# A decoder layer's cross-attention softmax taken in two halves of the batch

## What is computed

```python
def proj(x, W, bias):
    y = x @ W.T + bias
    return y.reshape(b, s, head_num, hd).transpose(0, 2, 1, 3).reshape(b * head_num, s, hd)
Q = proj(q, Wq, bq)
K = proj(k, Wk, bk)
V = proj(v, Wv, bv)
scores = jnp.einsum('bqd,bkd->bqk', Q, K) / jnp.sqrt(jnp.asarray(hd, jnp.float32))
attn = jax.nn.softmax(scores, axis=0)
res = jnp.einsum('bqk,bkd->bqd', attn, V)
out = res.reshape(b, head_num, s, hd).transpose(0, 2, 3, 1).reshape(b, s, hd * head_num)
```

## Time and profile before

| | us |
|---|---|
| median of 3 runs | 711.3 (708.06 to 711.74) |
| profiled execution | 712.35 |
| its span, first to last instruction | 710.6 |
| busy: PE / DVE / ACT / POOL | 652.4 / 557.7 / 460.2 / 419.3 |

### The profile page before, as it was taken

One profiled execution on the slowest core, in us unless ns is written; L12 is line 12 of the kernel. 1 busy time (PEld: TensorE's weight loads), 2 busy tenths in 40 slices (PEclk: granted clock), 3 DMA queues, 4 the chain that ended last, 5 costly groups with the idle time before them and its releaser, 6 DMA issues. The chain is left out here.

```text
span 710.6 us, 10958 instructions
## 1 busy us (share of the span) xinstructions
PE 652.4 (92%) x3298; PEld 450.0 (63%) x3298; DVE 557.7 (78%) x866; ACT 460.2 (65%) x1260; POOL 419.3 (59%) x366
## 2 busy tenths in 40 slices
...
DMA packets 29469, 56.46 MB, mean 79 GB/s; under 512 B 4705, under 2 KB 4961, under 8 KB 28898
## 3 DMA queue, kind: packets, MB, share of 16 engines
...
...
## 5 line engine op out<-in xcount | busy, mean ns | idle before, releaser
L1034 DVE SCALAR_TENSOR_TENSOR arena<-ps,arena 128x512 f32<-128x512 f32 x288 | 212.9, 746 | 16.7 <-PE ps L1382 4.7
L1382 PE MATMUL ps<-x_hi,w_sb 128*128 128x512 f32 x384 | 174.9, 455 | 16.9 <-DVE arena L1034 8.2
L1062 DVE SCALAR_TENSOR_TENSOR y<-ps,arena,y 128x512 f32<-128x512 f32 x192 | 138.9, 745 | 23.6 <-PE ps L1441 19.4
L1382 PE MATMUL ps<-x_lo,w_sb 128*128 128x512 f32 x384 | 154.2, 401 | 0.0
L1441 PE MATMUL ps<-heads_hi,wo_sb 128*128 128x512 f32 x256 | 110.6, 432 | 3.8 <-DVE y L1062 2.4
L754 ACT ACTIVATE arena<-ps,small 128x128 f32<-128x128 f32 x256 | 90.6, 377 | 36.2 <-DVE small L1040 36.2
L587 POOL TENSOR_TENSOR arena<-arena,consts 128x512 f32<-128x512 f32 x75 | 96.7, 1289 | 22.6 <-DMA arena<-arena 21.2
L581 POOL TENSOR_TENSOR arena<-arena,consts 128x512 f32<-128x512 f32 x75 | 96.8, 1291 | 22.2 <-DVE arena L1034 22.1
L1382 PEld LDWEIGHTS ps<-x_hi,w_sb 128*128 128x128 f32 x384 | 74.1, 193 | 51.4 <-issue 11.4
L605 POOL TENSOR_TENSOR y<-arena,y 128x512 f32<-128x512 f32 x64 | 82.4, 1288 | 39.4 <-ACT arena L795 37.3
L708 POOL TENSOR_SCALAR var_eps<-mean_var 128x2 f32<-128x2 f32 (+1 forms) x10 | 6.5, 647 | 166.0 <-DVE mean_var L1181 166.0
...
## 6 DMA issues: line engine op xcount, KB each, us to landing
arena<-arena SPq DMA_DIRECT2D x160, 128.0 KB, 2.3
...
```

Of the source, the lines that this page charges most:

```text
L1034: nc.vector.scalar_tensor_tensor(acc, group_bank(p, KC * c + g), scale_of(p // 2, c, g), acc, ALU.mult, ALU.add).then_inc(dve_scaled, 1)
L1062: nc.vector.scalar_tensor_tensor(dst, by_tile(out_bank(p, u)), out_scale_of(p // 2, u), dst, ALU.mult, ALU.add).then_inc(out_added, 1)
L1382: mm = nc.tensor.matmul(group_bank(p, u), w_sb[:, c, g, :], part[:, g, half * HALF:(half + 1) * HALF], start=(k == 0), stop=(k == 1))
```

## The change

Softmax in two halves. `maximum2(h)`, `shift(h)`, `add_exps(h)` do four batches. The first half is shifted by its own maximum. The second half's maximum is joined with the first's (a running maximum), and ACT makes one 128x128 factor `x_c`, the exponential of the difference, with which the first half's sum and, at the end, its inverse are multiplied. The two `tensor_reduce` of 2048 become `fold`: four `tensor_tensor` of 1024, 512, 256 and 128. PE no longer sums exponentials.

```diff
+            maximum2(0)
+            shift(0)
+            add_exps(0)
+            maximum2(1)
+            step(nc.vector.tensor_tensor(x_m[1], x_m[1], x_m[0], ALU.max))
+            nc.vector.tensor_tensor(x_c, x_m[0], x_m[1], ALU.subtract).then_inc(apart2_ready, 1)
+            shift(1)
+            dve.wait_ge(factor2_ready, 1)
+            step(nc.vector.tensor_tensor(x_s[0], x_s[0], x_c, ALU.mult))
+            add_exps(1)
+            step(nc.vector.tensor_tensor(x_s[1], x_s[1], x_s[0], ALU.add))
+            step(nc.vector.reciprocal(x_r[1], x_s[1]))
+            step(nc.vector.tensor_tensor(x_r[0], x_r[1], x_c, ALU.mult))
...
+            def fold(v, op, dst):
+
+                for n in (1024, 512, 256):
+                    step(nc.vector.tensor_tensor(v[:, 0:n], v[:, 0:n], v[:, n:2 * n], op))
+                step(nc.vector.tensor_tensor(dst, v[:, 0:P], v[:, P:2 * P], op))
```

```diff
+                        elif g == 0 and c in K2_TILES:
+                            wait_product_bank(f, f"G{KC * c}")
+                            channels_by_token(K2_TILES.index(c), wk2, ctx_t)
...
+                    elif c in K2_TILES:
+                        copy_k2(K2_TILES.index(c))
```

```diff
+            pe.wait_ge(out_added, DVE_TILES * QPK * 2 * NKV)
+            pe.wait_ge(part_added, QPK * 2 * NKV)
+            for n in range(KC):
+                turn_y(BPH + n)
+                next_unit(KC + n, wq2, x2_t)
+            pe.wait_ge(proj2_copied, 2 * KC)
             for b in range(BPH):
                 scores2(b)
+                turn_x(0, BPH + b)
+                next_unit(2 * KC + b, wk2, ctx_t)
+            pe.wait_ge(x_t_ready, NB)
+            for n in range(KC):
+                next_unit(3 * KC + n, wq2, x2_t)
...
+            for b in range(BPH):
+                scores2(BPH + b)
                 values(b)
+            for b in range(BPH, NB):
+                values(b)
```

```diff
+            copy_q2(12)
             exps2(0)
+            copy_q2(13)
+            seed_bias(0)
             exps2(1)
             exps2(2)
+            copy_q2(14)
+            seed_bias(1)
             exps2(3)
+            copy_q2(15)
+            seed_bias(2)
+            for b in range(BPH):
+                copy_scores2(BPH + b)
+                copy_v2(b)
+                seed_bias(b + 3)
+            act.wait_ge(apart2_ready, 1)
+            nc.scalar.activation(x_c, x_c, ACT.Exp, scale=XSCALE).then_inc(factor2_ready, 1)
```

354 lines of the change are left out of this document (176 added, 178 removed).

## The result

Of 20 runs of each kernel the median is 707.75 us (705.29 to 711.97) with the change and 710.83 us (706.88 to 714.39) before it. The ratio is 0.9962, 95% interval 0.9944 to 0.9981: a gain of 3.1 us, real but within the 0.5% that was called no change. The forecast was 702.2 us, so about 9 us of gain; a third of it came.

A forecast was written before the change was run, and what follows sets the result against it. Bound: PE's key and query units, then DVE's softmax, in a row, with DVE idle in the first. Span 710.6 - 10.1 + 1.0 = 701.5, plus 1.75 gives 703.25, less 1.05 gives 702.2 us; range 696.5 to 709.0.

The forecast's parts named there:

- Part 1: Last self-attention phase: four key units, 13.7 us of PE work, partly fill 3.5 us of gaps; phase ends 10.5 us later.
- Part 2: Last output products and first layer norm, `turn_y(0)` to `turn_y(4)`: 17.0 us, with DVE the slower engine at 14.3 us.
- Part 3: First half to its scores: four groups of scores, transposes and key unit take 19.5 us; PE later waits 2.3 us.
- Part 4: Second half: scores 4.42 us apart, then DVE alone for 26.8 us from the eighth copy; weighing starts 10.1 us earlier.
- Part 5: PE idle before `attend(0)`: the clock falls to half rate and costs 1.0 us, bounds 0 and 4.
- The check named at the end of the prediction: Prediction is wrong if the stretch from the last phase's end to `turn_y(4)` is far from 17 us.
- The bound of 19 us: Upper bound for the first layer norm stretch: each wait for POOL's deviation in full, 1.3 us, twice.
- a rival in which the clock stays down through the weighing: Half clock through the weighing and second layer norm adds 16 us: median 717.2 us, chance 0.05.
- the first rival: Last phase doesn't take in the key units and layer norm takes 19 us: 707.4 us, chance 0.12.

The follow-up runs named there:

- e1_ring: Changed kernel with the last 16 output products taking the four product banks in turn: `turn_y(4)` at 52.61 us after the last phase's first product instead of 55.48.
- e10_all_dve: Changed kernel with four product banks in turn, last query copy before the fourth exponential, values behind all scores, DVE's sums earlier around layer norm: 700.41 us, ratio 0.9836.
- e7_values_last: Changed kernel with the second half's scores in a row and all units of values behind them: from `turn_y(4)` to the weighing 95.63 us instead of 98.31.
- e4_behind: Changed kernel with the four key units moved from the last phase to behind it: weighing at 157.08 us after that phase's first product instead of 153.79.
- e8_bias_mm: Changed kernel with the values' bias put in by matmul instead of ScalarE's writes: weighing at 153.67 us after the last phase's first product instead of 153.79.
- e16_act_order: e10_all_dve with two bank sets for the second half's scores, three values' biases by matmul, ScalarE's exponentials ahead of copies of values: 694.1 us, ratio 0.9781.

## Why the prediction was wrong, by its own steps

The five steps, in us after the mark:

| step | forecast | measured | |
|---|---|---|---|
| Part 1, last values | +10.5 | +10.87 | right |
| Part 2, from `turn_y(0)` to `turn_y(4)` | 17.0 | 20.8 | 3.8 short |
| Part 3, four of scores, transposes, unit | 19.5 | 20.5 | 1.0 short |
| Part 3, wait before the fifth scores | 2.3 | 2.33 | right |
| clock behind that wait | 0 | 1.64 | missed |
| Part 4, three distances of scores | 13.3 | 14.2 | 0.9 short |
| Part 4, eighth copy to weighing | 26.8 | 26.25 | 0.55 over |
| Part 5, clock before `attend` | 1.0 | 0.5 | 0.5 over |

**Part 2 is the step that failed first.** Its sum, 14.3 us of DVE work and a last product through ACT and POOL, assumed that DVE works without a gap. It can do so only while PE's products run ahead by the ring, and the table of products gave one bank to five of them, so that PE waited for DVE (3.11 and 0.95 us) and then, at half clock, DVE for PE (1.31 and 2.45 us ahead of the sums at 508.63 and 512.68). The check named at the end of the prediction, a stretch far from 17 us, is what came. Undone by e1_ring (2.9 us) and by DVE's order in e10_all_dve (1.0 to 1.5 us), the stretch is 16.4 to 16.9 us, under the 17.0 that was forecast. The bound of 19 us didn't hold it either: it had a term neither for a bank that DVE must empty first nor for a clock that falls behind a 3.11 us wait. How the two share the 3.8 us no run shows.

**Part 5 looked for the clock at one place only,** the 13 us before `attend`, where it cost 0.5 us. It cost 1.64 us behind the 2.33 us wait, the wait that Part 3 had found and priced at its own length. Rows 7 had shown the clock fall behind PE's last work; that a short wait is enough wasn't read from any row. The trace of the kernel before has it: in the last phase, whose 0.93 stands in the earlier trace rows, the clock falls behind waits of 1.41 and 0.65 us (a product at 464.74 and the scores at 466.12). Windows there, columns as in the earlier trace rows:

```profile
466.00:468.00 2.00, 1.88 (x11) 1.71 (x12) 0.95 (x2) 0.00 (x0) 1.86 (x2) 0.78 0.97 332
468.00:470.00 2.00, 1.81 (x9) 1.51 (x7) 1.08 (x3) 1.95 (x9) 0.61 (x1) 0.50 0.44 180
```

The Trainium skill's page "TensorE: Matmul & The Clock Gate" says in its section on psum-queue depth-cycling that short idle times between groups of matmuls make the clock go to and fro. The changed kernel agrees: 0.50 in 570 to 572 behind one wait, 1.00 again from 574 on. In e7_values_last, with waits of 2.0 us between groups of 2.09, the clock didn't go to and fro but stayed at 0.50 from 576 to 592. I had used that section for a rival in which the clock stays down through the weighing (717.2 us); that one didn't come: the clock was 0.73 in 620 to 622 and 1.00 from 623 to 659.4.

**Parts 3 and 4 were short by the small seams.** 0.26 us for each group of the first half and 0.31 for each distance of the second come from taking instructions in a row at their issue time: a lone group of scores behind a unit takes 1.1 us until the next may start, not 0.99, and a unit between such groups 3.53 to 3.63, not 3.43. Four of the one and three of the other are 2 us. This is read from the rows alone; no run tests it.

**Right were** the size of the key units' part (e4_behind: 3.3 us, forecast 13.7 - 10.5 = 3.2), the fold (2.77 us against 2.85), and that DVE alone sets the way from the eighth copy to the weighing. The Trainium skill's page "VectorE: DVE Perf Modes" (section "The TRN2 errata") puts the widths 1024, 512 and 256 at an estimated 2.34 us; the row at 590.90 has 2.41 with two waits in it. The bias writes, which I took as a small gain, were none (e8_bias_mm).

The sum in one line: 3.8 + 1.0 + 1.64 + 0.9 - 0.55 and 0.5 of other rests makes the 7.3 us by which the weighing was late, and the smaller clock term gives 0.5 back. So of the forecast 9.1 us of span, 2.3 came. The banks (2.9), DVE's order (1.0 to 1.5) and the clock (1.64) are 5.5 to 6.0 of the 7.3 us, each with a run behind it.

The median of 707.75 lies beside the 707.4 of the first rival. That is luck: the rival had the key units unfilled, and e4_behind shows them filled. Only its second half came, a layer norm stretch of 19 us or more, and for another reason.

The forecast's mechanism, the two stretches overlapping, is nevertheless what e16_act_order shows: its weighing is 15.5 us ahead of the kernel before, more than the 10.1 that were forecast, because it also takes back two parts of the change itself, the units of values between the second half's scores and the one set of banks for them.
